# Two graph layers over 8192 nodes: the groups of ranked tiles redrawn, and the dense product over 28 node tiles in place of 32

## The reference

```python
h = relu(layernorm(x))                      # x: 8192 x 128, adj: 8192 x 8192, 0 or 1, with ones on the diagonal
H = h @ W.T + b                             # layer 0: attention over the neighbours
s, r = H @ a_s, H @ a_r
e = leaky_relu(A * s + A * r.T, 0.2)
x = x + softmax(where(A > 0, e, -9e15)) @ H
h = relu(layernorm(x))                      # layer 1: sum over the neighbours, then a maximum over them
p = relu(adj @ (h @ weight) + bias)
x = x + max over the neighbours of p
```

## Time and profile before

| | before |
|---|---|
| median of 3 executions | 2652.41 us (2651.3 to 2653.63) |
| profiled execution | 2656.13 us, of which the span of the instructions is 2654.4 |
| mean granted PE clock in it | 0.683 of full speed |
| busy: POOL | 1565.4 us (59%), 1620 instructions |
| busy: DVE | 1494.6 us (56%) |
| busy: PE | 990.8 us (37%) |
| busy: ACT | 379.5 us (14%) |

### The profile page before, as it was taken

One profiled execution on the slowest core, in us unless ns is written; L12 is line 12 of the kernel. 1 busy time (PEld: TensorE's weight loads), 2 busy tenths in 40 slices (PEclk: granted clock), 3 DMA queues, 4 the chain that ended last, 5 costly groups with the idle time before them and its releaser, 6 DMA issues.

```text
span 2654.4 us, 20418 instructions
## 1 busy us (share of the span) xinstructions
PE 990.8 (37%) x4772; PEld 571.1 (22%) x4772; DVE 1494.6 (56%) x4088; ACT 379.5 (14%) x1166; POOL 1565.4 (59%) x1620
## 2 busy tenths in 40 slices
PE   3664254444456654416469999400000000000000
PEld 1441143211234422416324444200000000000000
DVE  6888988888465564644665555176736741012211
ACT  1541054300223322214200000000000000000000
POOL 0001675027277757777466574377757777667776
PEclk8987677767777777657679999755555555555555
DMA  9999887579998997334432232422242222222121
GB/s 349 404 366 395 279 286 270 238 294 328 329 369 318 318 362 264 73 76 118 132 87 62 60 88 57 109 61 59 75 48 52 52 54 53 48 49 54 52 52 46
DMA packets 158194, 450.37 MB, mean 170 GB/s; under 512 B 34738, under 2 KB 82692, under 8 KB 125172
## 3 DMA queue, kind: packets, MB, share of 16 engines
q1 hardware_dynamic: 81972, 313.26, 31.5%
q0 software_dynamic: 53344, 114.94, 18.9%
q10 hardware_dynamic: 22752, 20.82, 2.5%
HBM read 409.76 MB, written 39.12 MB: 169 GB/s over the span
## 4 chain that ended last, share of the span: by engine, by line
POOL 40%; issue 17%; PE 15%; DVE 13%; DVEq 6%; DMA 5%; SPq 3%; POOLq 0%; ACT 0%; ACTq 0%
POOL ring L658 23%; PE psV L1070 13%; POOL ring L586 12%; DMA a_buf<-in_adj 3%; DVE words L1196 2%; DVEq L1195 2%; POOL out L664 2%; POOL y_table L599 1%; DVE words L1187 1%; DVE words L1191 1%; DVEq L1190 1%; SPq L400 1%; PE psV L899 1%; DVE found L1220 1%; SPq L387 1%
## 5 line engine op out<-in xcount | busy, mean ns | idle before, releaser
L586 POOL DMA_INDIRECT ring<-h_table,srec x523 | 512.1, 979 | 234.3 <-issue 157.1
L658 POOL DMA_INDIRECT ring<-p_table,srec x554 | 535.7, 967 | 189.0 <-issue 167.5
L1308 DVE TENSOR_TENSOR ring<-ring 128x128 f32<-128x128 f32 (+6 forms) x302 | 147.9, 490 | 560.1 <-DMA ring<-p_table,srec 405.1
L899 PE MATMUL psV<-a_buf,bit_ident 128*128 128x512 bf16 x1024 | 299.2, 454 | 245.4 <-DMA a_buf<-in_adj 175.4
L955 PE MATMUL psH<-ring,ident 128*128 128x128 f32 x1046 | 188.8, 355 | 294.3 <-ACT trec L754 136.2
L955 PEld LDWEIGHTS psH<-ring,ident 128*128 128x128 f32 x1046 | 178.9, 266 | 308.6 <-issue 241.8
L1070 PE MATMUL psV<-rec_all,a_buf 128*128 128x512 bf16 x1008 | 223.0, 380 | 0.0
L1080 PE MATMUL psH<-ones_row,flag_col 128*1 128x1 f32 x2 | 0.2, 163 | 587.2 <-DVEq L1537 587.2
L621 POOL DMA_INDIRECT ring<-y_table,srec x177 | 173.0, 977 | 56.6 <-issue 56.0
L899 PEld LDWEIGHTS psV<-a_buf,bit_ident 128*128 128x128 bf16 x1024 | 109.9, 110 | 418.6 <-issue 255.2
L572 POOL DMA_INDIRECT records<-rec_all,rank x63 | 63.2, 1003 | 165.4 <-DVEq L1273 146.8
(11 more groups left out here) (228 smaller groups left out, 2020.3 us busy)
## 6 DMA issues: line engine op xcount, KB each, us to landing
a_buf<-in_adj SPq DMA_DIRECT2D x256, 1024.0 KB, 12.0
ring<-p_table,srec POOLq DMA_INDIRECT x554
ring<-h_table,srec POOLq DMA_INDIRECT x523
packed<-wbuf ACTq DMA_DIRECT2D x32, 256.0 KB, 7.7
a_buf<-packed SPq DMA_DIRECT2D x8, 1024.0 KB, 6.4
trec<-records ACTq DMA_DIRECT2D x63, 128.5 KB, 3.3
h_table<-stage POOLq DMA_DIRECT2D x16, 258.0 KB, 8.0
a_buf<-r_row SPq DMA_DIRECT2D x1, 4096.0 KB, 18.9
```

Of the source, the lines that this page charges most:

```text
L586: pool.indirect_dma_start(ring[:, A_AT[q] + j, :], None, h_table, bass.IndirectOffsetOnAxis(srec_u[g][:, i, LIST + j:LIST + j + 1], 0)).th ...
L658: pool.indirect_dma_start(ring[:, C_AT[n] + j, 0:D], None, p_table, bass.IndirectOffsetOnAxis(slot, 0)).then_inc(s_rows[n % BUFS], 16)
L899: last = pe.matmul(psV[n % 2][:, h * BANK:(h + 1) * BANK].rearrange("p (g n) -> p g n", n=P), bit_ident[:, k, :], rows[:, :, k, :], start= ...
L1308: dve.tensor_tensor(ring[:, at:at + h, 0:D], ring[:, at:at + h, 0:D], ring[:, at + n - h:at + n, 0:D], op)
```

## The change

The groups are drawn again: 12 to 27, 1 to 11, 28 to 47 and 48 to 63 in place of 16 to 31, 1 to 15, 32 to 47 and 48 to 63. The stream of the adjacency follows them. With them change the slots (A, the gathers of h: 523 before, 518 after), the steps at which a group is ranked (15, 26, 46, 62), and the tables `STEP` and `BEHIND`; `LAST` goes from 83 to 77. The number of classes is now chosen for each group. The dense product takes 28 node tiles (7 batches), and 36 slot tiles are summed sparsely (198 gathers of y in place of 177). The third stage has 653 gathers in place of 662, and the segments stand behind tile 27. The hub's row keeps step 64 for its first part and has its sums and its norm a step earlier. Some buffers become aliases of others that are no longer in use. `LOADS` stays as it is.

```diff
-GROUPS = [(16, 16, 24), (1, 15, 48), (32, 16, 24), (48, 16, 24)]
-CLASSES = 32
+GROUPS = [(12, 16, 24), (1, 11, 48), (28, 20, 24), (48, 16, 16)]
+MOST = max(n for _, n, _ in GROUPS)
+CLASSES = [min(512 // n, 46) for _, n, _ in GROUPS]
...
-DENSE = 32
-DENSE_FROM = 31
+DENSE = 28
+DENSE_FROM = 27
...
+ENDS = [sum(n for _, n, _ in GROUPS[:g + 1]) - 1 for g in range(4)]
 LOADS = [15, 22, 40, 56]
...
-STEP = [19, 19, 20, 20, 21, 21, 22, 22, 23, 23, 24, 24, 25, 25, 26, 26, 39, 43, 45, 46, 47, 48, 49, 50, 51, 52,
+STEP = [18, 19, 19, 20, 20, 21, 21, 22, 22, 23, 23, 24, 24, 25, 25, 26, 33, 37, 38, 39, 40, 41, 42, 43, 43, 44,
...
-LAST = STEP[-1] + 2
+HUB_SCORES, HUB_SUMS, HUB_NORM = T, T + 8, T + 12
+LAST = max(STEP[-1] + 2, HUB_NORM + 1)
...
-HUB_SCORES, HUB_SUMS, HUB_NORM = T, T + 9, T + 13
-SPLITS = {HUB_NORM + 2: [4, 5, 6, 7], HUB_NORM + 4: [0, 1, 2, 3]}
+
+SPLIT_ORDER = [3, 4, 5, 6, 0, 1, 2] + list(range(7, BATCHES))
+SPLITS = {HUB_NORM + 2: 4, HUB_NORM + 4: 3}
+SPLIT_LAST = {0: 15, 4: 26, 7: 46, 12: 62}
...
-    return [m for m in range(len(Y_SLOTS)) if min((sum(Y_SLOTS[:m + 1]) + m + 8) * 9 // 32, 63) == step]
+    return [m for m in range(len(Y_SLOTS)) if min((sum(Y_SLOTS[:m + 1]) + m + 8) * 9 // 32, DENSE_BATCHES * BLOCKS - 1) == step]
...
-    ready = [sum(work) * min(sum(C_SLOTS[1:m + 2]) / sum(C_SLOTS[1:26]), 1) for m in (n - 1, n)]
+    ready = [sum(work) * min(sum(C_SLOTS[1:m + 2]) / sum(C_SLOTS[1:23]), 1) for m in (n - 1, n)]
...
-        REC = max(n * (LISTS + LIST + w) for _, n, w in GROUPS)
-        rec_all = sb("rec_all", [P, 2, REC])
+        rec_all = [sb(f"rec_all{i}", [P, max(n * (LISTS + LIST + w) for _, n, w in GROUPS[i::2])]) for i in range(2)]
...
-                if i % 4 == 0:
-                    for m, value in enumerate(y_stored(SPLIT_LAST[i // 4])):
+                if i in SPLIT_LAST:
+                    for m, value in enumerate(y_stored(SPLIT_LAST[i])):
...
-                if n in (16, 31, 47, 63):
-                    rank_rows((16, 31, 47, 63).index(n))
+                if n - 1 in ENDS:
+                    rank_rows(ENDS.index(n - 1))
...
-                for b in SPLITS.get(n, []):
+                for _ in range(SPLITS.get(n, 0)):
                     split_y(splits)
```

More of the change, by code:

```diff
@@ L38 @@
 STREAM = [t for a, n, _ in GROUPS for t in range(a, a + n)] + [0]
-TAKEN = {t: 48 if t < 3 else 40 if t < 5 else 32 if t < 14 else 24 if t < 47 else 16 for t in range(1, T)}
+TAKEN = {t: 48 if t < 3 else 40 if t < 5 else 32 if t < 12 else 24 if t < 47 else 16 for t in range(1, T)}
 WIDTH = {t: TAKEN[t] if t < 40 else 16 for t in range(1, T)}
@@ L283, in build @@
         flag_i = sb("flag_i", [1, 1], I32)
[L284 to L287, removed]
+        row_class = sb("row_class", [P, MOST])
+        one_hot = sb("one_hot", [P, BANK], BF16)
+        rank_f = sb("rank_f", [P, MOST])
+        rank = sb("rank", [P, 4, MOST], U32)
         e_raw = sb("e_raw", [P, 49])
@@ L472, in _ @@
             for i in range(2):
-                sp.wait_ge(s_pst[i], 16 * (DENSE_BATCHES // 2))
+                sp.wait_ge(s_pst[i], 16 * len(range(i, DENSE_BATCHES, 2)))
             sp.wait_ge(s_lowst, 16)
@@ L491, in _ @@
             sp.wait_ge(s_segst, 16 * 5)
-            sp.dma_start(seg_slots[:], segments.rearrange("(z p) k -> p z k", p=P)).then_inc(s_segin, 16)
+            sp.dma_start(seg_slots, segments.rearrange("(z p) k -> p z k", p=P)).then_inc(s_segin, 16)
             for z in range(HUB_TILES):
@@ L804, in dense_norm @@
                 act.wait_ge(s_hstep[l], t * 8 + 3)
-                act.activation(hub_nT[:], psF[:, 0:P], ACT.Copy).then_inc(s_hstep[l], 1)
+                act.activation(hub_nT, psF[:, 0:P], ACT.Copy).then_inc(s_hstep[l], 1)
                 act.wait_ge(s_hstep[l], t * 8 + 5)
@@ L951, in sum_slots @@
                     pe.wait_ge(s_att, q - 1)
-                pe.wait_ge(s_ranked, len([n for n in (15, 30, 46, 62) if n <= STEP[q]]))
+                pe.wait_ge(s_ranked, len([n for n in ENDS if n <= STEP[q]]))
                 pe.wait_ge(s_scaled, q + 1)
@@ L961, in count_classes @@
                 pe.wait_ge(s_onehot, g + 1)
-                closed = len([q for q in range(NR) if STEP[q] < (15, 30, 46, 62)[g]])
+                closed = len([q for q in range(NR) if STEP[q] < ENDS[g]])
                 if closed > 0:
                     pe.wait_ge(s_att, closed)
-                cols = one_hot[:, 0:CLASSES * n]
-                pe.matmul(psH[0][:, 0:CLASSES * n], upper_bf[:], cols, start=True, stop=True)
-                pe.matmul(psH[1][:, 0:CLASSES * n], ones_bf[:], cols, start=True, stop=True).then_inc(s_counted, 1)
+                m = CLASSES[g] * n
+                cols = one_hot[:, 0:m]
+                pe.matmul(psH[0][:, 0:m], upper_bf[:], cols, start=True, stop=True)
+                pe.matmul(psH[1][:, 0:m], ones_bf[:], cols, start=True, stop=True).then_inc(s_counted, 1)
             def turn_rows(n):
@@ L1400, in _ @@
                     mean_row()
-                if n in (15, 30, 46, 62):
-                    classify((15, 30, 46, 62).index(n))
+                if n in ENDS:
+                    classify(ENDS.index(n))
                 for q in AT_STEP[n]:
```

63 lines of the change are left out of this document (31 added, 32 removed), and 6 rows, old and new, of the table SLOTS.

## The result

Over 20 executions of each, the kernel before took 2652.01 us (median; 2648.07 to 2655.22) and the changed one 2657.24 us (2650.01 to 2661.49): ratio 1.0018, 95% interval 1.0011 to 1.0025. The change makes the kernel slower by about 5 us. The forecast was 2650.6, a little faster than before: the measured time lies inside the stated range (2635 to 2665), and the direction is the wrong one.

A forecast was written before the change was run, and what follows sets the result against it. The limit was taken to change by stage, POOL leading with 40% of the chain. Terms +20.0, -14.5 and -7.3 gave -1.8 (span 2652.6 against 2654.4); applied to the median 2652.41, the forecast was 2650.6 us, range 2635 to 2665.

The forecast's parts named there:

- +20.0 - 14.5 - 7.3: Forecast changes in us: start of the dense product, second stage (product and y gathers), third stage (POOL's p gathers).
- T0: Start of PE's dense product, ending the first stage: forecast 1371, 20 us later than 1351.1.
- the hub's y at 1314: First stage: hub scores end at 1242, then exponentials, sums and norm, 65.3 plus 6 us, give its y at 1314.
- The landing of the last ... I take 10: First stage: landing of the last of 46 POOL gathers before group 2, taken as 10 us, between 6 and 17.5.
- 865: First stage: time in us when group 2 is ranked, after an estimated 32 us of DVE work; POOL idles 38.
- 1092: First stage: time in us when group 3 is ranked, about 15 us after POOL's gathers and scatters end at 1077.
- 1144: First stage: time in us of group 3's first scores, 41 us earlier than 1185.5.
- 98, so 1242: First stage: the hub's eight score parts behind group 3's first scores take 98 us, ending at 1242, 36 later than before.
- The rank waits: First stage: POOL idles some 38 us before group 2's records and 15 before group 3's.
- In before eight were done among the last attention tiles: End of first stage: eight of 16 y splits ran in the loop before; now all 16 follow the hub, 2.7 us each.
- A rule weighed: First stage: DVE instructions with two SBUF inputs slow POOL's gathers, 0.94 to 1.07 us busy; costs 5 us of T0.
- The rival of the record load: First stage: group 2's record load, 45 us, holds SP's queue past its room; 15 us later, 2666; chance 0.26.

The follow-up runs named there:

- the sums' plan: Changed kernel with the second stage's sums placed at 8/32 of a block per gather or store, not 9/32: 2638.33 us, ratio 0.9932 to the kernel before.
- the eighth batch alone: Kernel before with seven batches of the dense product in place of eight and no slot tile added: 2613.41 us, ratio 0.9844 (chip E).
- The run with the hub's parts first: Changed kernel with the hub's eight score parts ahead of group 3's first scores, ten splits in the loop: 2621.92 us, ratio 0.9867 to the kernel before.
- the run with the late hub: Kernel before with the hub's score parts behind group 3's first scores and all splits behind the loop: ratio 1.0134 on chip B, 1.0038 on chip D.
- theory A of the repeated kernel before: Kernel before, unchanged, rerun on chip B (1.0000); its theory A: on slow chips engines stand still between instructions, so the difference lies in the first stage.
- the last version: Changed kernel with sums at 8/32, group 2's and group 3's ranks freed, hub's parts together ahead of group 3's scores: 2564.08 us, 0.9669 (B); 0.9676 (D).

## Why the prediction was wrong, by its own steps

**The sign failed on one term.** The sum was +20.0 - 14.5 - 7.3; the profiles have +27.9 - 16.3 - 9.7. The last two were right in mechanism and within 2.5 us. In the third stage the new idle before the first segment gather is there, 3.9 us (2198.1) for the 4 forecast, though the trace names no releaser for it. That POOL and not PE would end the second stage is shown by the sums' plan and by the eighth batch alone; 16.3 of PE's 42.1 us came in, for a forecast of 14.5. The step that failed is T0, "the hub's y at 1314" and "T0 = 1371, 20 us later": the delay was there and its cause right, but it was sized too small: it measured 27.9. With 20.0 in its place and the other two terms as measured the sum would be -6.0, a faster kernel. (1314 and the 57.5 behind it are 1371.5; the sum went on with 1371.1.)

**Where the 8 us arose.** "The landing of the last ... I take 10": it took 16.6 (POOL's 46 gathers from 540.9 end at 598.6, the scores begin at 615.2), nearly the 17.5 of the earlier trace rows, though no record load was beside it. What long landings have in common here is the long row of gathers: 46 and 47 of them, with 185 and 146 GB/s moved in the wait, while the last of tile 17's 24 landed in 6.8 us at 350 GB/s. A cause is not shown. With the sums that made POOL go on at 644.1, not 639. The chain ran behind its forecast by 8.0 at group 2's rank ("865": 873.0), 14.2 at group 3's ("1092": 1106.2), 9.3 at the first scores ("1144": 1153.3) and 14.2 at the end of the hub's scores ("98, so 1242": 102.9, so 1256.2). The hub's tail gave back 10 (62.2 to its y, forecast 72), and from there to T0 it took 60.7 for 57.5. So the errors went both ways, more of them late, and the net 8 was more than the 1.8 us by which the sum was faster.

**The rank waits** (38 and 15 us forecast, 41.8 and 20.1 measured) are shown to be DVE's order of work for group 2: moving scores behind the extraction removed the wait and 35 us. For group 3 the reason is read from the traces and only in part shown by a run.

**The hub's parts behind group 3's scores**, with the splits behind the loop, are shown to cost 34 us of T0. That the change paid some of that with group 3's 28.5 us head start is argued, not measured apart.

**"In before eight were done among the last attention tiles"** is true of the order. It is not a price: taking the eight out costs 6.7 us of T0, not their 23.

**A rule weighed.** Gathers had 40.51 / 43 = 0.94 us each ahead of the hub's parts (windows of POOL's L587: us, busy, clock, DMA share, GB/s). Beside the parts the mean depends on the window: 1.03 in the one shown, 30.04 / 24 = 1.25 from 1160 to 1200.

```profile
920.00:980.00 60.00, 40.51 (x43) 0.77 1.02 361
...
1210.00:1250.00 40.00, 24.62 (x24) 0.57 0.30 71
```

The run with the hub's parts first settles what it goes with. There DVE works the parts one after the other, one each 5.16 us, and three of POOL's issues fill the same time, two long and one short. The long ones lie beside L1343 and L1346, the two instructions of a part that take two operands from SBUF; the short one lies beside the reduction (L1348), which takes one:

```profile
1146.71 1.71 POOL L587 DMA_INDIRECT ring<-h_table,srec  x1 [0.30 <-issue]
1148.72 1.60 POOL L587 DMA_INDIRECT ring<-h_table,srec  x1 [0.30 <-issue]
1150.62 0.95 POOL L587 DMA_INDIRECT ring<-h_table,srec  x1 [0.31 <-issue]
...
1146.37 1.23 DVE L1343 SCALAR_TENSOR_TENSOR V<-V 128x1024 f32<-128x1024 f32 x1
...
1148.27 1.23 DVE L1346 TENSOR_TENSOR a_buf<-a_buf,V 128x1024 f32<-128x1024 f32 x1
1149.57 1.22 DVE L1348 TENSOR_REDUCE hub_m<-a_buf 128x1 f32<-128x1024 f32 x1
```

In the changed kernel's own trace, from 1135 to 1256, 31 of POOL's indirect DMAs lie beside such an instruction of DVE's (L1304 is another), with a mean of 1.47 us and 21 of them over 1.2; the 55 others have 0.96, and none is over 1.2. That bears out the rule of the Trainium skill (GPSIMD Engine Reference, 1. Specifications) that VectorE instructions with two SBUF inputs contend with GpSimd. What it costs in T0, 5 us by the prediction, no run measures by itself.

**The rival of the record load** did not come: SyncE held it 19.4 us, not 45.

```profile
671.05 19.44 SPq L401 DMA_DIRECT2D rec_all<-h_table  x1
```

**From spans to medians.** A second miss adds to the first. The forecast took 3.7 us off for the distance of one execution from the median. With 20 executions, that of the kernel before was 4.1 above its median, that of the changed one 1.1. So 3 of the 5.2 us between the medians are not in the two traces. On chip B the profiled spans differ by 0.7 (2653.0 and 2653.7) and the medians by 6.5. In which stage those executions differ stays open.

## What to carry to other kernels

When work leaves the engine that ends a stage, look at once at what the plan of the next engine was tuned to: here a factor 9/32 had no price before the change, took over half of the 42 us of the eighth batch after it (23), and cost one character to mend. Where several engines run one written order, ask of each item not only how long it takes but what it stands behind: pieces of DVE work of 5.5 us that need no gathers were put behind scores that wait for them, and DVE stood idle for 21 us just ahead of both. Look one engine further as well: put ahead of the scores, they still stood behind closes that waited for ACT, and ACT for a load that stood too early in its order. And where a forecast lies 2 us from no change, and its largest term is a long chain of estimates, its sign says little.

## What was not expected of the hardware

On two of the chips (C and D) every kernel took 11 to 14% longer, with instructions about as long as elsewhere (the median gather of p 0.947 us on D and 0.944 on B, in the changed kernel). The waits of DVE in the changed kernel on chip D, and on chip B (engine, line, releaser: us in total, times, longest):

```profile
DVE l_inv L1320 <- remote: 95.1, 10, 28.4
DVE rec_all L1445 <- remote: 59.3, 5, 22.1
DVE rec_all L1445 <- PE psV L1072: 55.4, 19, 8.6
...
DVE words L1189 <- issue: 41.7, 7, 24.1
```

```profile
DVE e_raw L1288 <- DMA ring<-h_table,srec: 160.2, 27, 23.1
...
DVE l_inv L1320 <- PE psH L957: 31.5, 5, 16.7
```

On D the engines stand still up to 28 us for a release that the trace calls remote, or for nothing that it shows ("issue"), and seven batches of the product, with the wait up to the first gather of p, took 375 us in place of 327. There the changed kernel was 1.9% faster, 57 us. The traces say roughly in which stage. From T0 to the end the changed kernel took 1393.4 us on D, and the kernel before 1410.5 (its last two stages, from the run with the late hub): 17 us of the 57. The rest, some 40 us by subtraction, lies ahead of T0, where on chip B the change loses 30. So on D it is the first stage that turns the sign, the place that theory A of the repeated kernel before names; its reason is not shown. No trace of the kernel before itself was taken there, and what the waits are was not found. The finding of 0.2% holds for the first kind of chip only, and that of the last version, 3.2 to 3.3%, for one of each.
